# Test-time-training scan on one core: target and key rows turned in place in the projection stage, output variance and transpose moved within a chunk, three output buffers

## What is computed

```
xn = layernorm(groupnorm(x) as tokens)
XQ = rope(xn @ q_w.T); XK = rope(xn @ k_w.T); XV = xn @ v_w.T      # per head
eta = token_idx * sigmoid(xn @ lr_w + lr_b) / 32
# scan over 64 chunks, carry W1 (32x32 per head and image) and b1:
Z1    = xk @ W1 + b1
grad  = layernorm-l2-backward(Z1, target = xv - xk, g, bb)
Z1bar = xq @ W1 - eta * tril(xq @ xk.T) @ grad + b1 - tril(eta) @ grad
W1   -= (last_eta * xk).T @ grad;  b1 -= sum(last_eta * grad)
out   = xq + layernorm(Z1bar) * g + bb
x = x + layernorm(out) @ o_w.T
```

## Time and profile before

| what | value |
|---|---|
| time, median of 3 (lowest, highest) | 668.66 us (667.87 to 670.31) |
| the profiled execution | 668.61 us, span 666.8 us |
| TensorE busy | 524.4 us, 79% |
| VectorE busy | 474.6 us, 71% |
| ScalarE busy | 363.8 us, 55% |
| GpSimd busy | 341.0 us, 51% |
| TensorE clock granted in the scan | 0.50 of full speed |

### The profile page before, as it was taken

The page is one execution under the profiler, slowest core; times in us unless marked ns, Lnnn a source line. Parts: engine busy times, 40 slices in busy tenths (PEclk is TensorE's granted clock), DMA queues, the critical chain, the costliest instruction groups (busy, mean ns, idle before and its releaser), DMA issues. The chain is left out here.

```text
span 666.8 us, 29820 instructions
## 1 busy us (share of the span) xinstructions
PE 524.4 (79%) x12150; PEld 365.0 (55%) x12150; DVE 474.6 (71%) x1484; ACT 363.8 (55%) x1172; POOL 341.0 (51%) x595
## 2 busy tenths in 40 slices
PE   0399999997558877878778887788687599859997
PEld 0143334434457767777777777777675245444552
DVE  6456777664558888989888998899997267528441
ACT  0424444223447676777767778777675276544432
POOL 0368888776234545555455554555653456421333
PEclk9999999998555555555555555555555699979999
DMA  8101111112910000000000000000004200000212
GB/s 346 55 5 39 39 38 38 32 31 49 219 38 3 0 0 1 0 1 0 0 1 1 0 0 0 1 0 0 0 3 180 94 1 0 1 1 4 74 67 111
DMA packets 9862, 24.66 MB, mean 37 GB/s; under 512 B 1845, under 2 KB 2510, under 8 KB 9550
## 3 DMA queue, kind: packets, MB, share of 16 engines
q1 hardware_dynamic: 9806, 24.01, 11.6%
HBM read 11.42 MB, written 4.19 MB: 23 GB/s over the span
## 5 line engine op out<-in xcount | busy, mean ns | idle before, releaser
L781 PE MATMUL PS<-work 32*32 32x32 f32 x4064 | 83.7, 238 | 58.8 <-DVE work L955 52.3
L781 PEld LDWEIGHTS PS<-work 32*32 32x32 f32 x4064 | 79.9, 152 | 70.0 <-issue 67.1
L770 PE MATMUL PS<-work 64*32 64x64 f32 x2048 | 69.4, 310 | 19.0 <-ACT work L1098 15.1
L500 PE MATMUL PS<-X,work 128*128 (+3 forms) x160 | 72.0, 597 | 7.0 <-ACT X L640 6.4
L1035 POOL TENSOR_TENSOR work<-work 128x128 f32<-128x128 f32 x64 | 25.5, 398 | 86.9 <-DVE work L955 75.8
L770 PEld LDWEIGHTS PS<-work 64*32 64x32 f32 x2048 | 55.6, 164 | 26.0 <-issue 24.8
L793 PE MATMUL PS<-work 32*64 32x32 f32 x2016 | 68.1, 292 | 0.8 <-issue 0.8
L793 PEld LDWEIGHTS PS<-work 32*64 32x64 f32 x2016 | 59.6, 216 | 5.0 <-issue 1.0
L1027 POOL TENSOR_TENSOR work<-work,mask 128x256 f32<-128x256 f32 x64 | 46.6, 728 | 15.0 <-ACT work L1130 8.3
L500 PEld LDWEIGHTS PS<-X,work 128*128 128x128 f32 (+1 forms) x160 | 25.9, 169 | 48.0 <-issue 47.2
L423 ACT ACTIVATE X<-X,par (+1 forms) x16 | 12.1, 806 | 70.4 <-DVE X L416 70.4
(11 more groups left out here) (145 smaller groups left out, 1309.1 us busy)
## 6 DMA issues: line engine op xcount, KB each, us to landing
X<-in_x SPq DMA_DIRECT2D x4, 1024.0 KB, 8.1
TK<-KP SPq DMA_DIRECT2D x64, 64.0 KB, 1.9
X<-QP SPq DMA_DIRECT2D x8, 512.0 KB, 9.0
TK<-in_x SPq DMA_DIRECT2D x4, 1024.0 KB, 9.3
out<-TK SPq DMA_DIRECT2D x16, 256.0 KB, 2.2
work<-in_rope SPq DMA_DIRECT2D x2, 512.0 KB, 9.9
cst<-in_consts SPq DMA_DIRECT2D x1, 289.0 KB, 4.9
work<-in_wk SPq DMA_DIRECT2D x1, 256.0 KB, 11.3
```

What stands on the lines that cost most here:

```text
L500: mm = nc.tensor.matmul(o, lhs(j), xt(i, j), start=(j == 0), stop=(j == J - 1))
L770: mm = nc.tensor.matmul(PS[HD * a:HD * a + HD, ZB[p], b * ZW:b * ZW + ZW], KT2[p][r:r + 64, k * B + b, :, :].rearrange("p e t -> p (e t)") ...
L781: mm = nc.tensor.matmul(PS[HD * a:HD * a + HD, bank, b * width:b * width + HD], AM[p][HD * a:HD * a + HD, b, part, :, :].rearrange("p e t ...
```

## The change

The packed buffer TKH and `rows_of` go. Behind `finish_target` a new `turn_rows` turns the targets and the keys of the finished block in place, so that each chunk's 32 columns (2 x 16 tokens) by 32 channels become 32 token rows. TS and `khx` read TK directly through `head_rows`. `out_var(c-2)` and `out_turn(c-4)` move from between ZC and TS to behind GL(c), ahead of `out_rows(c-1)`. ZQ gets a third buffer. GpSimd does masks before `out_norm`. VectorE's projection loop is written out. The last loads of x wait for the last `khx` instead of the last `rows_of`.

```diff
+                def turn_rows(i):
+                    dve.wait_ge(s_ttf, i * J + J)
+                    for s in range(2):
+                        rows = TK[:, :, s, i * BLK:(i + 1) * BLK].rearrange("p e (c t) -> p c e t", t=CS)
+                        nc.vector.transpose(rows, rows)
...
                     if not first:
                         finish_target(i - 1)
+                        turn_rows(i - 1)
...
-                body(0, True)
-                with dve.Fori(1, NBLK - 2) as i:
-                    body(i, False)
-                body(NBLK - 2, False)
-                body(NBLK - 1, False)
+                for i in range(NBLK):
+                    body(i, i == 0)
...
                 finish_target(NBLK - 1)
+                turn_rows(NBLK - 1)
...
-        TKH = [carve(2, B, HD) for _ in range(2)]
-        ZQ = [carve(B, HD) for _ in range(2)]
+        ZQ = [carve(B, HD) for _ in range(3)]
...
+            def head_rows(s, c):
+
+                return TK[:, :, s, :].rearrange("p e (b n) -> p b e n", b=B)[:, :, :, c * CS:(c + 1) * CS]
...
-                def rows_of(c, p):
-
-                    if past(c, 2):
-                        dve.wait_ge(q["khx"], c - 1)
-                    nc.vector.transpose(
-                        TKH[p].rearrange("p s b d -> p (s b d)"),
-                        TK[:, :, :, :].rearrange("p e s (b n) -> p (s b) e n", b=B)[:, :, :, ds(c * CS, CS)]
-                    ).then_inc(q["tkh"], 1)
...
                 def out_rows(c, p):
 
                     dve.wait_ge(q["attn"], c + 1)
-                    if past(c, 2):
-                        dve.wait_ge(q["zn"], c - 1)
-                    nc.vector.tensor_tensor(ZQ[p], PS[:, QB[p], 0:B * HD].rearrange("p (b d) -> p b d", b=B),
+                    if past(c, 3):
+                        dve.wait_ge(q["zn"], c - 2)
+                    nc.vector.tensor_tensor(ZQ[c % 3], PS[:, QB[p], 0:B * HD].rearrange("p (b d) -> p b d", b=B),
                                             Bs[p], ALU.add).then_inc(q["zq"], 1)
...
-                    if past(c, 2):
-                        out_var(c - 2)
-                    if past(c, 4):
-                        out_turn(c - 4)
                     dve.wait_ge(q["sd"], c + 1)
-                    dve.wait_ge(q["tkh"], c + 1)
-                    nc.vector.tensor_tensor(TS, TKH[p][:, 0, :, :], bc(sd1), ALU.mult).then_inc(q["ts"], 1)
+                    nc.vector.tensor_tensor(
+                        TS.rearrange("p b (e t) -> p b e t", e=E), head_rows(0, c),
+                        sd1.unsqueeze(2).unsqueeze(3).broadcast_to([P, B, E, CS]), ALU.mult).then_inc(q["ts"], 1)
...
-                    if not is_last(c):
-                        rows_of(c + 1, 1 - p)
+                    if past(c, 2):
+                        out_var(c - 2)
+                    if past(c, 4):
+                        out_turn(c - 4)
                     if past(c, 1):
                         out_rows(c - 1, 1 - p)
...
                     pool.wait_ge(q["gl"], c + 1)
+                    if not is_last(c):
+                        masks(c + 1, 1 - p)
                     if past(c, 3):
                         out_norm(c - 3, 1 - p)
-                    if not is_last(c):
-                        masks(c + 1, 1 - p)
...
                 def khx(c, p):
-                    act.wait_ge(q["tkh"], c + 1)
+                    if past(c, 2):
+                        act.wait_ge(q["upd"], c - 1)
                     for e in range(E):
-                        kx = nc.scalar.activation(KHX[p][:, :, e, :], TKH[p][:, 1, :, :], ACT.Copy,
-                                                  scale=upd_mask[:, e:e + 1])
+                        kx = nc.scalar.activation(
+                            KHX[p][:, :, e, :].rearrange("p b (f t) -> p b f t", f=E), head_rows(1, c), ACT.Copy,
+                            scale=upd_mask[:, e:e + 1])
...
-                sp.wait_ge(q["tkh"], NC)
+                sp.wait_ge(q["khx"], NC)
```

More of the change, by code:

```diff
@@ L719, in build @@
         with nc.Block() as block:
-            names = ("init wcopy bcopy kt2 qt2 qr kr tkh khx base qbase corr s1 am z p sq ss sz zc v sd r ts y yp m u u2 "
+            names = ("init wcopy bcopy kt2 qt2 qr kr khx base qbase corr s1 am z p sq ss sz zc v sd r ts y yp m u u2 "
                      "yl c w yc gl upd attn zq sqq ssq sdq rq zn zt ot").split()
@@ L955, in body @@
                     nc.vector.tensor_tensor(GL[p], WX, YC, ALU.add).then_inc(q["gl"], 1)
-                    if not is_last(c):
-                        rows_of(c + 1, 1 - p)
+                    if past(c, 2):
+                        out_var(c - 2)
+                    if past(c, 4):
+                        out_turn(c - 4)
                     if past(c, 1):
                         out_rows(c - 1, 1 - p)
-                rows_of(0, 0)
                 for c in range(NC):
@@ L1034, in out_norm @@
                         pool.wait_ge(q["zt"], c + 0)
-                    nc.gpsimd.tensor_tensor(ZN, ZQ[p], bc(sdq[1 - p]), ALU.mult).then_inc(q["zn"], 1)
+                    nc.gpsimd.tensor_tensor(ZN, ZQ[c % 3], bc(sdq[1 - p]), ALU.mult).then_inc(q["zn"], 1)
                 def body(c, p):
@@ L1136, in out_square @@
                     act.wait_ge(q["zq"], c + 1)
-                    nc.scalar.activation(SQQ, ZQ[p], ACT.Square).then_inc(q["sqq"], 1)
+                    nc.scalar.activation(SQQ, ZQ[c % 3], ACT.Square).then_inc(q["sqq"], 1)
                 def out_sd(c, p):
```

## The result

| what | before (beside it) | after |
|---|---|---|
| time, median of 4 (lowest, highest) | 669.03 us (667.87 to 670.31) | 658.63 us (655.9 to 660.29) |
| the profiled execution | 668.61 us, span 666.8 us | 655.9 us, span 654.1 us |
| VectorE busy | 474.6 us | 464.2 us |

The ratio is 0.984, 95% interval 0.9802 to 0.9878: 10.4 us faster, where 14.8 were forecast. The profiled execution of after is the fastest of its four; a second profile of the same kernel (first experiment), of an execution at the median, has a span of 656.8 us.

The account below looks back on a forecast made before the run. The scan, half the span, was taken as bound by VectorE's 4.10 us chain plus 1.10 us waiting for TensorE per chunk. Scan -22.4 and projection stage +7.6 made -14.8 us: 653.8 us, range 647.5 to 662.

Parts of the forecast that it names:

- both parts: Part 1, scan: chain shortened, -22.4 us. Part 2, projection stage: sixteen new transposes, +7.6 us.
- the hole grew over 1.10 us: Sign of being wrong: VectorE's stretch from a chunk's last gradient add to next Z1, set by TensorE, exceeds 1.10 us.
- The chain gets 0.38 us shorter.: Scan, VectorE: without out_var and out_turn, ZC to the add behind TS takes 0.77 instead of 1.15 us; 59 chunks, -22.4 us.
- 0.42 us are left, so it is not the next bound.: Scan, TensorE: its chain from correction to last query product ends 0.42 us before its next start would come.
- The turns cost 7.6 us in the projection stage.: Two 128 x 1024 transposes per block, 1.30 us each; delays into blocks 2 to 7 plus the last pair, +7.6 us.
- The last pair costs its own length, 2.5 us.: End of projection stage: the last two transposes follow the final L561 with nothing later to cover them, 2.5 us.
- work in the hole is free before 1.10 us: Scan: VectorE work between last gradient add and next Z1 costs nothing up to 1.10 us; moved work ends at 0.86.
- (a): Scan: TS reading in runs is dear, or another wait takes the freed time; 0.13 us a chunk, +7.8, 661.6 us; 14%.
- (b): Scan's start: VectorE's longer written-out code is refilled late, one wait of 5.2 us, 659.0 us; 5%.
- (c): Projection stage: transposes take 2.4 us each, start-up paid for every 128 elements; +15.1, 668.9 us, no difference; 8%.
- (d): Projection stage: transposes collide with GpSimd, 17.5 us more plus 6.5 for held GpSimd ropes, 677.8 us; 7%.
- (e): Better: delays of blocks 2 to 5 vanish in slack (-4.4) and early chunks gain (-1.5), 647.9 us; 4%.

Follow-up runs that it names:

- first experiment: The changed kernel with no edit, timed in more rounds and profiled once more: 658.61 us, ratio 0.9835 to the kernel before.
- scan's part alone: Kernel before, with out_var and out_turn behind the gradient, three ZQ buffers and masks before out_norm; rows_of and the projection stage stay: 650.88 us, ratio 0.9722.
- loop of four: Changed kernel, with TensorE's scan loop taking four chunks an iteration instead of two: 655.76 us, ratio 0.98 to the kernel before.
- turns in the gaps: Changed kernel, with the sixteen transposes moved into VectorE's idle time (before later ropes, before the rates' copy, behind the scan's second chunk): 649.91 us, ratio 0.9716.
- written-out version of after: Changed kernel, with TensorE's scan loop written out: 680.75 us, ratio 1.0172; the same edit in the kernel before: 681.42 us, ratio 1.0177.
- turns in the gaps with the loop of four: Changed kernel, with the transposes in VectorE's idle time and TensorE's scan loop over four chunks: 649.86 us, ratio 0.9702 to the kernel before.

## Why the prediction was right, and where its size was off

The direction, the mechanism and both parts held, and the time lies in the range. The forecast was 4.8 us too low against the median, 2.1 us against the profiled execution, which happened to be a good one. In the second profile, at the median, the 4.8 us lie as follows: 1.2 more than forecast up to the first gradient, 1.3 less in chunks 0 to 4, 3.7 more from there to chunk 63, and 1.2 more behind it. One of the prediction's own signs of being wrong did come: the hole grew over 1.10 us, in every second chunk.

1. *The chain gets 0.38 us shorter.* Right: L919 to L933 is 0.77 us, 0.88 us of moved work fit under the hole (0.86 forecast), and no wait for GpSimd is left. The scan's part alone shows that this and the third buffer are the whole gain.
2. *"0.42 us are left, so it is not the next bound."* This is the step that failed. The 0.42 us were slack of TensorE's products. Behind them TensorE's loop returns every second chunk and starts no sooner than 0.6 us after its last product, so every second hole grew by 0.21 us, and the period by 0.09, L913 being 0.12 shorter. Held against before chunk by chunk, the 26 returns in front of chunks 8 to 58 make 1.8 us of the 2.7 that chunks 4 to 63 fell short (19.7 for 22.4). Another 0.6 is chunk 6, where TensorE also waits for issue (0.9 us, before 0.6). In the second profile the returns are again 1.8, of 3.7. That the long holes are the returns, the loop of four showed. The profile before could not show the return, since it lay under VectorE's longer chain; that the list has a branch there could be read from the code.
3. *The turns cost 7.6 us in the projection stage.* Right in total: TensorE's first products behind the barrier start at 172.30 for 164.65, +7.65 (rows below). GpSimd's first rope operation is 0.2 us later in blocks 0 and 1, and in blocks 2 to 7 by 1.2, 2.2, 3.5, 4.8, 5.3 and 5.3 us: steps of 1.0, 1.0, 1.3, 1.35, 0.45 and 0.0 for a forecast of 1.0, 1.0, 1.0, 1.4, 0.7 and 0. One turn is 1.22 us for 1.30, a pair 2.37 for 2.4.
4. *The last pair costs its own length, 2.5 us.* It does up to the barrier, but 0.7 us more come behind it (8.36 less 7.65), a term that the sum lacks. In after, TensorE's clock is lower when the scan starts. The windows of after (PE, PEld, DVE, ACT, POOL busy, granted clock, DMA share, GB/s):

```profile
166.00:168.00 2.00, 1.76 (x116) 1.59 (x104) 0.16 (x1) 0.00 (x0) 0.00 (x0) 1.00 0.00 0
168.00:170.00 2.00, 0.00 (x0) 0.00 (x0) 1.97 (x4) 0.00 (x0) 0.00 (x0) 1.00 0.03 8
170.00:172.00 2.00, 0.00 (x0) 0.00 (x0) 1.99 (x2) 0.00 (x0) 0.00 (x0) 0.66 0.00 0
172.00:174.00 2.00, 1.62 (x6) 1.35 (x6) 0.00 (x0) 0.55 (x3) 1.65 (x4) 0.50 0.65 131
```

TensorE's first products of the scan, of after and then of before:

```profile
172.30 1.19 PE L759 MATMUL PS<-small,cst 128*128 128x128 f32 x4 [4.54 <-PEq L441]
```

```profile
164.65 0.68 PE L751 MATMUL PS<-small,cst 128*128 128x128 f32 x4 [2.12 <-PEq L441]
```

In after they come behind 4.54 us idle, run at a granted clock of 0.50, the 1.2 GHz level, and take 1.19 us; before, behind 2.12 us, they run at full clock, the 2.4 GHz level, and take 0.68. With the turns in the gaps it is so again:

```profile
164.94 0.68 PE L761 MATMUL PS<-small,cst 128*128 128x128 f32 x4 [2.13 <-PEq L441]
```

But the longer wait does not by itself decide the level. Two profiles have it the other way round, the written-out version of after and the turns in the gaps with the loop of four:

```profile
172.96 0.68 PE L759 MATMUL PS<-small,cst 128*128 128x128 f32 x4 [4.52 <-PEq L441]
```

```profile
165.00 1.19 PE L761 MATMUL PS<-small,cst 128*128 128x128 f32 x4 [2.15 <-PEq L441]
```

Four of the five profiles with the long wait begin the scan at 0.50, and one of the seven with the short one. Nor is the clock always high before the wait: before, it was 0.50 from 160 to 162 us, with TensorE at work, and rose while it idled; in after it was 1.00 from 166 to 168 and fell while it idled. So the 0.7 us are what the lower level costs these products; that the last pair brings it about is likely but not shown. From start to start, 0.46 of the 0.7 us are in the first four and 0.24 in the two behind them.

5. *What the sum did not ask.* Both terms were priced, but not whether the second was needed for the first. The prediction said itself that work in the hole is free before 1.10 us; by the earlier trace rows an L876 behind the others adds 0.44 less an overlap of 0.1 to the 0.86. That is 1.2 us, 0.1 over the hole, and in the run of the scan's part alone not even this showed in the period. So 7.6 us were paid for next to nothing.
6. *The rivals.* (a) fell: TS is 0.28 us and waited once from 200 to 500 us, 0.2 us, for ScalarE. (b) did not occur on VectorE, but written-out code on TensorE brought it. (c) and (d) fell: 1.22 us a turn, and GpSimd's rope operation beside them keeps its mean, 1374 ns in both kernels. (The Trainium skill, "SBUF — State Buffer", section Who interferes with whom, does not name transposes among what contends; this trace agrees: the pair takes 2.37 us at 68.59 us, beside GpSimd, and 2.37 at 169.62, where GpSimd is idle.) (e) was half right: chunks 0 to 4 did gain 1.5 us, and 1.3 in the second profile (28.22 and 28.40 us for 29.71). But the scan's part alone and the turns in the gaps, with the same steps moved, have 29.29 and 29.02, so how much of that gain is the change's is not shown.

What stays open is why these first chunks vary (TensorE waits for issue there in every version), and why L913 and the hole trade so exactly in the scan's part, whose hole is 0.05 us longer at the same period.

## What to carry to other kernels

Price a move by the slack that it moves into, on every engine, and count an engine's loop return as work of that engine: it shows as nothing until the slack is gone. Ask of each part of a change whether the others need it, and run the parts alone: here one half brought 18.7 us and the other lost 8.0. Work done once per block costs its length if it stands between an engine's last and next dependent step, and nothing if it is dropped into a gap that already exists.

## What the runs showed of the hardware

- At a return of TensorE's loop some 0.6 us lie between its last product and the next (0.63 in the loop over two chunks, 0.58 in that over four), where without a return it is 0.30 to 0.42, set by the wait for the gradient. The same chunks written out cost 22.1 and 11.9 us, at 1.56 instead of 0.38 MB of instructions.
- A 128x1024 in-place transpose in runs of 16 takes 1.22 us, where eight of 128x128 at 0.296 us make 2.4: what each small one pays at its start is paid about once. GpSimd beside it makes no difference (2.37 us a pair either way).
- An operation of VectorE with two SBUF operands can take longer beside GpSimd: ZC takes 0.53 us in the steady chunks, beside GpSimd's L1008, and 0.28 in the first chunk of after, where GpSimd is idle; the product L913 takes 0.41 us beside the copy L1016 and 0.29 where it starts when that is nearly over.
- The same four products at the scan's start took 1.19 us at a granted clock of 0.50 and 0.68 at 1.00. Both levels were seen behind a wait of 4.5 us and behind one of 2.1 us, so that wait alone does not tell the level.
